# Router dot products and row means taken from the transposed scan output by TensorE, output products written in place, statistics spread over more places

## The reference

```python
x = x + s6(layernorm(x))          # x is (16, 1024, 512): 16 batches of 1024 tokens
x = x + ffn(layernorm(x))
# s6, for each batch, d of 512 and n of 16, with t over 1024 tokens:
delta = softplus(d_rank @ dt_proj_w.T + dt_proj_b)
h[t]  = exp(delta[t] * A[d, n]) * h[t-1] + delta[t] * x[t] * Bm[t, n]
y[t, d] = sum_n h[t, d, n] * Cm[t, n] + x[t, d] * D[d]
# ffn: weights = x @ router_w + router_b picks 127 tokens of each batch by top-k;
# attention and an MLP run on those alone, the other tokens pass through.
```

## Time and profile before

| | us |
|---|---|
| median of 3 runs | 4442.13 (4439.07 to 4443.27) |
| profiled execution, own time | 4437.25 |
| its span, first to last instruction | 4435.3 |
| scans, first start to last end | 80.9 to 3423.8 |
| DVE / POOL / ACT / PE busy, share of the span | 85% / 76% / 64% / 69% |

### The profile page before, as it was taken

The page is one execution under the profiler, slowest core; times in us unless marked ns, Lnnn a source line. Parts: engine busy times, 40 slices in busy tenths (PEclk is TensorE's granted clock), DMA queues, the critical chain, the costliest instruction groups (busy, mean ns, idle before and its releaser), DMA issues. The chain is left out here.

```text
span 4435.3 us, 53118 instructions
## 1 busy us (share of the span) xinstructions
PE 3074.1 (69%) x17574; PEld 1397.1 (31%) x17574; DVE 3769.6 (85%) x3027; ACT 2854.0 (64%) x4425; POOL 3364.4 (76%) x1716
## 2 busy tenths in 40 slices
PE   4666666666666666676675767576664289999997
PEld 1223232322222222222232323232222145555553
DVE  2999999999999999999999999999998755555552
ACT  5777777777778687878777777777774223332321
POOL 3999999999999999999999999999998200000010
PEclk7767676767677776767777767676776599999998
DMA  4454546463646455554545464636453300000000
GB/s 102 105 134 124 144 115 162 97 171 82 177 96 162 110 148 129 129 134 124 135 124 144 116 161 97 168 81 181 92 147 76 145 22 20 19 19 19 19 19 8
DMA packets 198113, 471.95 MB, mean 106 GB/s; under 512 B 60688, under 2 KB 61200, under 8 KB 197088
## 3 DMA queue, kind: packets, MB, share of 16 engines
q1 hardware_dynamic: 177136, 452.11, 40.4%
q0 software_dynamic: 20736, 16.88, 1.4%
HBM read 126.83 MB, written 73.43 MB: 45 GB/s over the span
## 5 line engine op out<-in xcount | busy, mean ns | idle before, releaser
L951 POOL TENSOR_TENSOR ch<-hid,cmat 128x1024 f32<-128x1024 f32 x1024 | 2386.2, 2359 | 73.4 <-DVE hid L817 61.8
L817 DVE TENSOR_TENSOR_SCAN hid<-place,inp 128x1024 f32<-128x1024 f32 x1024 | 2266.7, 2271 | 81.8 <-ACT place L667 81.1
L667 ACT ACTIVATE place<-delr,a_neg 128x1024 f32<-128x1024 f32 x1024 | 1127.7, 1112 | 291.7 <-DVE hid L817 188.2
L440 PE MATMUL ps_y<-ch,nsum 128*32 128x256 f32 x8192 | 869.3, 522 | 452.9 <-POOL ch L951 451.4
L806 DVE TENSOR_TENSOR inp<-place,bmat 128x1024 f32<-128x1024 f32 x816 | 941.7, 1212 | 65.4 <-ACT place L673 63.6
L451 PE MATMUL ps_y<-ident,ysb 128*128 128x128 f32 x1024 | 314.2, 403 | 543.2 <-ACT ysb L680 543.2
L440 PEld LDWEIGHTS ps_y<-ch,nsum 128*32 128x32 f32 x8192 | 249.9, 137 | 1070.5 <-POOL ch L951 832.3
L913 POOL TENSOR_TENSOR inp<-dxr,bmat 128x1024 f32<-128x1024 f32 x208 | 489.9, 2356 | 0.0
L451 PEld LDWEIGHTS ps_y<-ident,ysb 128*128 128x128 f32 x1024 | 226.0, 273 | 755.8 <-ACT ysb L680 731.3
L1212 POOL DMA_INDIRECT out_rows<-row,idx_out x16 | 41.1, 2570 | 532.3 <-issue 298.4
L435 PE MATMUL ps_y<-xhT,dskip 128*32 128x256 f32 x2048 | 259.4, 597 | 138.7 <-ACT xr L687 138.7
(11 more groups left out here) (176 smaller groups left out, 4208.5 us busy)
## 6 DMA issues: line engine op xcount, KB each, us to landing
dxr<-dxT SPq DMA_DIRECT2D x1024, 128.0 KB, 2.4
delr<-delT SPq DMA_DIRECT2D x1024, 128.0 KB, 2.4
xr<-in_x SPq DMA_DIRECT2D x32, 1024.0 KB, 6.4
bmat<-b_and_c SPq DMA_DIRECT2D x256, 128.0 KB, 3.4
cmat<-b_and_c SPq DMA_DIRECT2D x256, 128.0 KB, 3.1
x_rows<-xr SPq DMA_DIRECT2D x16, 2048.0 KB, 8.2
out_rows<-xr SPq DMA_DIRECT2D x32, 1024.0 KB, 4.5
w<-in_w SPq DMA_DIRECT2D x2, 4096.0 KB, 23.9
```

Source lines behind the costliest of these rows:

```text
L440: last = pe.matmul(ps_y[q * CH:(q + 1) * CH, 0:2 * P], nsum[:], ch[:, g, q * 2 * P:(q + 1) * 2 * P], start=False, stop=(g == GROUPS - 1))
L667: nc.scalar.activation(place[:, PLACE[par, c, g], :], delr[:, c % 2, :], ACT.Exp, scale=a_neg[:, i:i + 1])\
L817: nc.vector.tensor_tensor_scan(hid[:, g, :], place[:, PLACE[par, c, g], :], inp[:, g, :], 0.0, ALU.mult, ALU.add).then_inc(hid_ready, 1)
L951: nc.gpsimd.tensor_tensor(ch[:, g, :], hid[:, g, :], cmat[:, g, :], ALU.mult).then_inc(ch_ready, 1)
```

## The change

- **Router.** The weights that project `xhat` (`xproj`) get 32 more columns, all the router's weights; row 96 of `xpT` is then the dot product of the normalised row. PE turns that row into columns (`router_x`, 8 small matmuls at (14, 0)). All 16 chunks' `ysb` are kept, and PE multiplies each by an 8-column matrix (`router_y`, 32 matmuls with 128x128 weights and 8 moving columns), which gives the dot products with `y` and the sums of `y`. ACT copies both (`copy_router_y`, at (1, 3)), and POOL forms the mean of the new rows (`make_mean2`, (1, 3)) and the router weights (`route`, (5, 0), five operations). DVE's `router`, ACT's row sums for the second layernorm and the copy of the weights are gone.
- **In place.** POOL writes the product over `hid`; `scan` (c, g) now waits for PE's sum of (c-1, g), and POOL waits for the scan alone.
- **Inputs.** POOL makes the group-3 input for chunks 2 to 12 only; DVE makes those of 1 and 13 again.
- **Places.** ACT's eight squares of the second layernorm stand in pairs at (2, 1) to (3, 0), `make_out` at (3, 3) to (4, 1), the `add_terms` of k=2 move from (0, 2)-(1, 2) to (1, 3)-(2, 2), `SUMS1` begins at (5, 0), and `ln2_finish` and one `delta` step are at (3, 1).

```diff
-SUMS1 = {(5, 3): range(0, 3), (6, 0): range(3, 6), (6, 1): range(6, 9), (6, 2): range(9, 13), (6, 3): range(13, 17)}
+SUMS1 = {(5, 0): range(0, 1), (5, 1): range(1, 2), (5, 2): range(2, 3), (5, 3): range(3, 5), (6, 0): range(5, 7),
+         (6, 1): range(7, 10), (6, 2): range(10, 13), (6, 3): range(13, 17)}
+SQUARES2 = {(2, 1): (0, 1), (2, 2): (2, 3), (2, 3): (4, 5), (3, 0): (6, 7)}
...
+ROUTE_Y = {(0, 1): range(0, 4), (0, 2): range(4, 6), (0, 3): range(6, 11), (1, 1): range(11, 14), (1, 2): range(14, 16)}
+COPY_ROUTE_Y = (1, 3)
...
-OWN_AT = tuple(range(1, 14))
-ROUTED = (4, 2)
+OWN_AT = tuple(range(2, 13))
+ROUTED = (5, 0)
...
-        ysb = sb("ysb", [P, 2 * P])
+        ysb = sb("ysb", [P, CHUNKS, 2 * P])
...
+            def router_x(b):
+                aux_free(b, ("route_x",))
+                for t in range(TC):
+                    last = pe.matmul(aux[:, t:t + 1], xpT[R + 2 * N:P, t * P:(t + 1) * P],
+                                     ident[R + 2 * N:P, R + 2 * N:R + 2 * N + 1], start=True, stop=True)
+                last.then_inc(aux_full, 1)
+            def router_y(b, cs, emptied):
+                if 0 in cs:
+                    pe.wait_ge(aux_emptied, emptied)
+                for c in cs:
+                    for t in range(2):
+                        last = pe.matmul(aux[:, 8 * t:8 * t + 8], ysb[:, c, t * P:(t + 1) * P], rw_chunk[:, c, :],
+                                         start=(c == 0 and t == 0), stop=(c == CHUNKS - 1 and t == 1))
+                last.then_inc(route_y_full, 1)
...
+            def copy_router_y(b):
...
+                act.wait_ge(route_y_full, b * len(ROUTE_Y) + (len(LAST_ROUTE_Y) if is_last(b) else len(ROUTE_Y)))
...
                 if has(b, 1) or c > 0:
-                    dve.wait_ge(ch_ready, tile(b, c, g) - GROUPS + 1)
+                    dve.wait_ge(ch_summed, tile(b, c, g) - GROUPS + 1)
...
-                for t in range(4 * h, 4 * h + 4):
-                    if has(b, 1) or t > 0:
-                        dve.wait_ge(router_sum, b * TC + t)
-                    nc.vector.scalar_tensor_tensor(junk[:], xr[:, par, t, :], m2[:, 1, t:t + 1], aux[:],
-                                                   ALU.add, ALU.mult, accum_out=r2[:, 8, t:t + 1])\
...
+            def make_mean2(b, par):
+                pool.wait_ge(route_y_copied, 2 * b + 2)
...
-                        if has(b, 1) or c > 0:
-                            pool.wait_ge(ch_summed, tile(b, c, g) - GROUPS + 1)
-                        nc.gpsimd.tensor_tensor(ch[:, g, :], hid[:, g, :], cmat[:, g, :],
+                        nc.gpsimd.tensor_tensor(hid[:, g, :], hid[:, g, :], cmat[:, g, :],
                                                 ALU.mult).then_inc(ch_ready, 1)
```

More of the change, by code:

```diff
@@ L77 @@
 NUSE = len(USES)
-LN1 = 5
-LN2 = 7
+LN1 = 6
+LN2 = 6
+ROUTE_STEPS = 4
 LN_ACT = 20
+LN2_ACT = 11
 ZSTEPS = 3
@@ L419, in add_terms @@
                     aux_free(b, ("s", k, h))
+                    if (k, h) == (2, 0) and has(b, 1):
+                        pe.wait_ge(route_y_copied, 2 * b)
                     pe.wait_ge(z_act, b * KD * ZACT + k * ZACT + ZACT)
@@ L481, in body @@
                                     step_size(b + 1, k, h)
+                        if (c, g) in ROUTE_Y and has(b, 1):
+                            router_y(b - 1, ROUTE_Y[c, g], b * NUSE + USE["z", 2, 1] + 1)
+                        if (c, g) == (CHUNKS - 1, 1) and final:
+                            router_y(b, LAST_ROUTE_Y[0], nb_run * NUSE)
+                        if (c, g) == ROUTE_X and not final:
+                            router_x(b + 1)
                         for (k, h), at in ADD_TERMS.items():
@@ L679, in copy_y @@
                     act.wait_ge(yt_ready, b * CHUNKS + c)
-                nc.scalar.activation(ysb[:], ps_y[:, 0:2 * P], ACT.Copy).then_inc(ysb_ready, 1)
+                if c in ROUTE_READ and has(b, 1):
+                    act.wait_ge(route_y_full, (b - 1) * len(ROUTE_Y) + ROUTE_READ[c])
+                nc.scalar.activation(ysb[:, c, :], ps_y[:, 0:2 * P], ACT.Copy).then_inc(ysb_ready, 1)
             def copy_x1(b, par, c):
@@ L699, in _ @@
             act.wait_ge(eps_ready, 1)
+            nc.scalar.activation(squares[:, 1, 1], rw[:], ACT.Identity, accum_out=rw_sum[:]).then_inc(rw_summed, 1)
+            act.wait_ge(rw_summed, 1)
             ln1_sums(0, 0, range(17))
@@ L787, in _ @@
             copy_x1(last, 1, CHUNKS - 1)
-            copy_rw(last, nb_run * NUSE)
-            ln2_sums(last, 1, range(17))
+            copy_router_y(last)
+            ln2_squares(last, 1, range(TC))
             for t in range(TC):
@@ L847, in body @@
                         scan(b, par, c, g)
-                    if has(b, 1) and c in ROUTER:
-                        router(b - 1, other, ROUTER.index(c))
                     for g in range(GROUPS):
@@ L860, in _ @@
             batches(body)
-            last = nb_run - 1
-            for h in range(2):
-                router(last, 1, h)
             dve.wait_ge(wt_ready, 1)
@@ L869, in _, with newton @@
         def _(pool):
-            def newton(b, m, r, chain, chain_act, per):
-                pool.wait_ge(chain_act, b * LN_ACT + LN_ACT)
+            def newton(b, m, r, chain, chain_act, per, made):
+                pool.wait_ge(chain_act, made)
                 n = b * per
@@ L963, in body @@
                         if (c, g) == ROUTED and has(b, 1):
-                            route(b - 1)
+                            route(b - 1, 1 - par)
+                        if (c, g) == MEAN2 and has(b, 1):
+                            make_mean2(b - 1, 1 - par)
+                        if (c, g) == SCALE_ROUTE_X and not final:
+                            scale_route_x(b + 1, 1 - par)
                     if c + 1 in OWN_AT:
@@ L971, in _ @@
                     delta(0, 0, k, step)
+            scale_route_x(0, 0)
             batches(body)
+            make_mean2(nb_run - 1, 1)
             ln2_finish(nb_run - 1)
-            route(nb_run - 1)
+            route(nb_run - 1, 1)
     return out_done
```

181 lines of the change are left out of this document (121 added, 60 removed).

## The result

The changed kernel takes 4458.0 us (median of 17 runs, 4426.88 to 4479.55), the kernel before 4442.25 us (18 runs, 4434.53 to 4445.6): a ratio of 1.0029, 95% interval 1.0015 to 1.0042. An eighteenth run of the changed kernel, in a slow state, took 5651.21 us; it is left out, and with it the median would be 4458.6. I had forecast 4371 us; the change makes the kernel slower by 0.3%. The profiled execution of the changed kernel took 4462.77 us, its span is 4460.7 us. Its runs also scatter over 52.7 us where those of before scatter over 11.1, and the shorter ones tend to have the higher granted clock: 4426.88 us at a mean of 0.777, 4479.55 at 0.760.

What follows compares the result with a forecast made beforehand. DVE and POOL were both taken as full; 199.6 us of DVE work plus 5.3 of waits gave period 204.9, 4.8 less. Fourteen batches plus the ends: 71 us off, 4371 us; own range 4352 to 4392, eight in ten 4335 to 4420.

Steps and rivals of the forecast that it cites:

- Router matmuls on PE: Chunks 0 and 1: 64 router passes a batch at 0.135 us each, costing about 0.1 us at the scan of (2, 0).
- my bounds 0.135 and 0.26: Price of a router pass in us: below from a half-clock group sum with 32-column weights, above from `turn_y`.
- rival B: Chunks 0 to 2: PE's chain holds every batch, waits 13.4 us, period 213, +48 us, 4485 us; chance 0.09.
- rival A: Chunks 3 and 7 lose their waits, only POOL's floor holds: period 202.5, 4337 us; chance 0.17.
- Rival D: `make_mean2` behind (1, 3) holds POOL's queue: 2 us there and 2 in chunk 3, period 209, no change; chance 0.06.
- Rival C: Chunks 4 to 7: next batch's rows come late, waits 2 to 3 us more, period 207.5, 4408 us; chance 0.18.
- The squares: Chunk 3: ACT's eight squares ahead of the decay of (3, 2) give DVE a new wait of 1.9 us.
- Chunks 5 to 7: `make_out` burst costs about 0.3 us; chunk 7's wait of 1.9 us shrinks to about 1.1.
- The write in place: At (0, 3): the scan waits for PE's sum, a new wait of 1.3 us a batch.
- DVE's own length: Whole batch: 11 chunks of 12.11 and 5 of 13.27 us, 199.6 us DVE must do alone.
- POOL's floor: Whole batch: 85 large products at 2.315 us and 19 small operations, 202.0 us, so no period under about 202.
- The ends: Batch 0 +1 us, batch 15 -3, behind the last scan -3.7 (row sums gone), start +1.5.

Runs made afterwards that it cites:

- The first experiment: The changed kernel with router_y doing one chunk of each piece, 20 passes a batch instead of 64: 4412.98 us, ratio 0.9936.
- The second: The changed kernel with every router_y matmul moving 128 columns of the identity instead of 8 of weights, router weights meaningless: 4401.49 us, ratio 0.991.
- the fifth experiment: The changed kernel with the eight router-weight columns moved 16 times over, 128 moving columns a pass, whole computation done: 4400.9 us, ratio 0.9908.
- the wide kernel: The kernel of the fifth experiment: the changed kernel with router weights moved 16 times over, 128 moving columns a pass: 4400.9 us, ratio 0.9908.
- the sixth experiment: The wide kernel with the first statistics' sums (SUMS1) back in the places of the kernel before: 4411.43 us, ratio 0.9935.
- the third experiment: The kernel before with only the product written over hid, scan waiting for PE's sum: 4443.1 us, ratio 1.0001.
- The version with the input in chunk 13: The wide kernel with POOL, instead of DVE, making one group's input in chunk 13 too: 4377.46 us, ratio 0.9867.

## Why the prediction was wrong

What the forecast made of the profiled executions was -71 us; it was +25.5. The miss of 96 us is, from the two traces: 80 in the middle batches (a period of 210.6 us where I had 204.9), 13 behind the last scan, 3 in batches 0 and 15. The waits of DVE make most of the 80: they are 10.1 us a batch where I had 5.3, and DVE's own length adds 0.9.

- **"Router matmuls on PE" is the step that failed.** I took 0.135 us a pass, "since it is nearer in work: the moving columns are few". The passes measured 0.213 at the half clock and 0.11 at the full one, which is what a pass of 128 columns takes. In chunks 0 and 1, mostly at the half clock, the upper of my bounds 0.135 and 0.26 was the nearer, and the row to scale from was `turn_y`, whose weights have 128 columns too. Its own pace in the kernel before was 0.213 (from 1551.46 to 1552.31 four passes start); my 0.26 took in the end of the last pass:

```profile
1551.46 0.64 PE L452 MATMUL ps_y<-xr,ident 128*128 128x128 f32 x2
1551.88 0.63 PE L451 MATMUL ps_y<-ident,ysb 128*128 128x128 f32 x2
1552.31 0.63 PE L452 MATMUL ps_y<-xr,ident 128*128 128x128 f32 x2
```

The term that followed from the price, 0.1 us at the scan of (2, 0), became waits of 1.86 us a batch in chunk 2, and chunk 3's came out at 3.89 instead of 1.9. The first experiment shows that 44 of the 64 passes are worth some 40 us. The rule of the Trainium skill that I set beside it (TensorE: Matmul & The Clock Gate, LDWEIGHTS: a load of 128 columns costs 107 ns) agrees with 0.11 at the full clock, and not with 0.213 at the half one. I wrote that it spoke against the change; by my own figures it did not, since its 6.8 us a batch are less than the 8.6 of my 0.135, and the 0.9 beside it should be 1.0.

- **The clock was taken from the row of the old instructions.** Against rival B I put the 0.88 of chunk 1, "before with the same `add_terms` there". But the change takes all twelve passes of `add_terms` out of chunk 1, to chunk 2, and puts narrow router passes in, and the clock there became 0.57 on average. A granted clock belongs to what an engine does in the stretch; move that, and the row no longer holds. The second and the fifth experiment show that the low clock, with the same passes, costs some 57 us by the medians and 54 by the ratios. What brought it down, the going of `add_terms` or the coming of the narrow passes, no run takes apart: none moves `add_terms` back. That it is 0.60 with a third of the passes points to the former. The rule I quoted beside rival A (the Trainium skill, TensorE: Matmul & The Clock Gate, What's actually happening: busy stretches raise the clock) does not describe chunk 1 of batch 2, where PE is busy for 12.12 of 12.12 us at a granted clock of 0.50.
- **Rival B was the right mechanism**, at a quarter of its strength: in four batches of fourteen the chain from PE through ACT's queue holds DVE 7 us longer (2.0 us of the period), in the others the half clock ends in time. The sign I had named for it, DVE waiting for PE in chunks 2 and 3, did not come: DVE waits for ACT, which waits for PE. **Rival D's** wait is there too, 3.45 us per batch ahead of `make_mean2`, in the long batches up to 7.8; POOL's queue behind it loses little in the usual batches, since POOL waits for DVE 3.95 us in chunk 13 anyway, where I had 1.8. **Rival C's** sign came, waits for decays in chunks 5 and 6, but not its cause: over batches 1 to 14 ACT waited for the load of the rows once, 0.7 us.
- **The squares.** I had 1.9 us in chunk 3; it is 3.9 on average, 5.1 in the long batches, 3.4 in the others (2.7 in batch 7) and 1.4 to 1.6 once the clock is high. In batch 7 the start of that chain was right: `copy_x1` of chunk 1 ends 34.7 us behind the batch's start, where I had 34.5. It ends 33.7 us behind it in the wide kernel, whose wait is the shorter, and 43.7 us behind it in batch 2, where each of ACT's copies had waited for PE.
- **Chunks 5 to 7** were set at 0.3 + 1.1 us. They cost 0.24 + 0.94 + 1.89. The spread of the sums is not to blame, as the sixth experiment shows; that ACT is behind by the sums, the copies of the rows and the decays together is argued, no run takes them apart.
- **The write in place** was nearly right: 1.3 us forecast, 0.84 found, 1.1 alone in the kernel before, where it cost no time.
- **DVE's own length** was 199.6 and is 200.5 us (200.51 us of busy time in batch 7, or the period less its idle time). The difference is 13 us over the middle batches, of many small pieces, which I did not take apart.
- **POOL's floor** was not reached, and was put 1.3 us too high: 202.0 forecast; 64 + 11 + 10 large products and the small ones are 200.7 us of busy time in batch 7. But a floor says nothing of when. In the chunks with its own input POOL was the faster engine and stood idle 3.96 us at chunk 13; there one more input fits, and in chunk 1 it does not.
- **What the high clock leaves.** The profiled execution of the wide kernel, 4403.47 us, is still 37 us above the 4366 of the forecast: 28 in the middle batches (a period of 206.9 us), of DVE's own length and the waits in chunks 5 to 7, and 9 behind the last scan. The clock and the passes are not the whole miss.
- **The ends.** I had -3.7 us behind the last scan. The statistics of the last rows are ready 4.6 us later instead, by the row of 56 router passes, for which I had put down "four matmuls", the last piece only. The other 5 us were lost later, 3 of them some 120 us behind the last scan. There PE waits 2.65 us, which is new, and 1.61 where it was 0.44, and the same sixteen matmuls take 3.78 instead of 2.05 us. First the kernel before, then the changed one:

```profile
3547.76 2.05 PE L1347 MATMUL ps_m<-onehot,GT 128*128 128x128 f32 x16 [0.44 <-DVE GT L1684]
```

```profile
3569.07 0.66 PE L1366 MATMUL ps_m<-identf,qk 128*128 128x128 f32 x4 [2.65 <-DVE qk L1763]
3571.33 3.78 PE L1440 MATMUL ps_m<-onehot,GT 128*128 128x128 f32 x16 [1.61 <-DVE GT L1777]
```

The kernel before with nothing but the write in place (the third experiment) shows the same waits, and its part behind the last scan is 6.1 us longer than in the kernel before. The version with the input in chunk 13, which has the router's change, does not show them (1010.7 us behind the last scan, before 1011.5). So these waits are not the router's; why DVE's `qk` is late in some profiled executions stays open. The rows of the third experiment:

```profile
3549.53 0.66 PE L1270 MATMUL ps_m<-identf,qk 128*128 128x128 f32 x4 [2.87 <-DVE qk L1667]
3551.80 3.78 PE L1344 MATMUL ps_m<-onehot,GT 128*128 128x128 f32 x16 [1.61 <-DVE GT L1681]
```

## What to carry to other kernels

Here a pass of few moving columns over freshly loaded weights took as long as one of 128, so price it from the row with the same weights, and read the pace from the starts. When a change gives an engine other work in a stretch, its clock in that stretch is unknown again: forecast both levels, and weigh the queue that stands behind the engine at the lower one, for a copy that waits in the order ahead of the critical work costs all of its lateness beyond the slack behind it (a wait of 4.94 us made a scan 2.95 us late in batch 2, one of 4.12 us none in batch 7). Idle time on a full engine has a place: the same 2.36 us of work gained 23 us in one chunk and lost 35 in another.

## What the runs showed of the hardware

- With 128-column fp32 weights a pass of 8, 32 or 128 moving columns takes the same time: 0.11 us at the full clock, 0.213 at the half (128 columns: 925 passes at the full clock, 22 at the half; the first pass of a row mostly took 0.21 at the full clock too).
- The number of moving columns went with the granted clock, at an unchanged number of loads and passes: in chunk 1 it was 0.57 with 8 columns (0.60 with 8 columns and a third of the passes), 0.78 with 32, and 1.00 with 128. In the kernel with 8 columns the profile has PE busy 12.12 of 12.12 us in chunk 1 of batch 2, at 1.2 GHz throughout.
- More work made the kernel faster: with sixteen times the columns in the router passes 4400.9 instead of 4458.0 us, a ratio of 0.9908 instead of 1.0029.
